# Windowed attention and feed-forward on one core: maxima from tiles of 32 queries of four heads, maxima and sums turned by VectorE, o stored by quadrant

## What is computed

```python
q = (x @ Wq.T).reshape(Bb, Tt, H, HD).transpose(0, 2, 1, 3)
k = (x @ Wk.T).reshape(Bb, Tt, H, HD).transpose(0, 2, 1, 3)
v = (x @ Wv.T).reshape(Bb, Tt, H, HD).transpose(0, 2, 1, 3)
attend = (|i - j| <= 128) | (i == 0) | (j == 0)
logits = where(attend, einsum('bhqd,bhkd->bhqk', q, k) / sqrt(HD), -inf)
out = einsum('bhqk,bhkd->bhqd', softmax(logits), v)
return out @ Wo.T
```

## Time and profile before

| | us |
|---|---|
| median of 3 runs | 1153.32 |
| lowest, highest | 1152.99, 1154.62 |
| span of the profiled execution | 1152.4 |
| attention, first shift row to last (L1347) | 193.0 to 759.1 |

### The profile page before, as it was taken

The page is one execution under the profiler, slowest core; times in us unless marked ns, Lnnn a source line. Parts: engine busy times, 40 slices in busy tenths (PEclk is TensorE's granted clock), DMA queues, the critical chain, the costliest instruction groups (busy, mean ns, idle before and its releaser), DMA issues.

```text
span 1152.4 us, 26576 instructions
## 1 busy us (share of the span) xinstructions
PE 1126.9 (98%) x9115; PEld 785.0 (68%) x9115; DVE 979.5 (85%) x3169; ACT 843.4 (73%) x1513; POOL 706.8 (61%) x935
## 2 busy tenths in 40 slices
PE   9999997999999999999999999999999999999998
PEld 8888884455555555555555455558888988898887
DVE  7889857899889998899889999867888888888885
ACT  7989983788888888888788888875465546554654
POOL 3665565677778777887778877773344334433443
PEclk9999998999999999999999999999999999999999
DMA  6999897555555555545565554240232113211201
GB/s 199 295 296 281 257 266 168 114 131 118 137 133 122 132 125 136 132 115 137 126 138 130 114 138 108 68 139 29 74 102 64 56 55 102 64 55 56 74 20 37
DMA packets 158166, 145.24 MB, mean 126 GB/s; under 512 B 21564, under 2 KB 157776, under 8 KB 158032
## 3 DMA queue, kind: packets, MB, share of 16 engines
q1 hardware_dynamic: 158032, 143.54, 48.8%
HBM read 91.74 MB, written 50.95 MB: 124 GB/s over the span
## 4 chain that ended last, share of the span: by engine, by line
PE 73%; DVE 7%; issue 2%; ACT 1%; POOL 1%; DVEq 0%; POOLq 0%; ACTq 0%
PE e_psum L1549 15%; PE e_psum L1503 15%; PE e_psum L1527 14%; PE e_psum L1844 6%; PE e_psum L1846 5%; PE e_psum L1267 3%; PE e_psum L1825 3%; PE e_psum L1824 3%; DVE n_stats L142 2%; DVE f_x L1958 2%; PE e_psum L1829 1%; PE e_psum L255 1%; PE e_psum L254 1%; PE e_psum L253 1%; PE e_psum L1793 1%
## 5 line engine op out<-in xcount | busy, mean ns | idle before, releaser
L1665 DVE CUSTOM_DVE_ANT_0 a_masked<-e_psum,band 128x387 f32<-128x387 f32 (+1 forms) x1024 | 493.3, 534 | 58.8 <-PE e_psum L1503 55.8
L1622 ACT ACTIVATE a_weights<-e_psum 128x1024 f32<-128x1024 f32 (+1 forms) x512 | 398.0, 806 | 87.2 <-PE e_psum L1527 82.2
L1401 POOL TENSOR_SCALAR_AFFINE_SELECT a_weights<-a_weights 128x1024 f32<-128x1024 f32 x256 | 276.2, 1091 | 59.9 <-ACT a_weights L1622 58.7
L1503 PE MATMUL e_psum<-e_k,e_q 96*128 96x387 bf16 (+1 forms) x1024 | 281.4, 327 | 3.0 <-PEq L281 1.4
L1888 POOL TENSOR_TENSOR f_square<-f_relu 128x512 f32<-128x512 f32 x128 | 146.1, 1142 | 209.6 <-ACT f_relu L1877 198.6
L1527 PE MATMUL e_psum<-e_q,e_k 128*128 128x384 bf16 (+2 forms) x1408 | 255.6, 279 | 1.5 <-ACT a_weights L1622 1.1
L1549 PE MATMUL e_psum<-a_weights,a_v 128*17 128x384 f32 (+2 forms) x2816 | 195.8, 392 | 1.0 <-POOL a_weights L1401 1.0
L1527 PEld LDWEIGHTS e_psum<-e_q,e_k 128*128 128x128 bf16 x1408 | 129.0, 98 | 95.6 <-issue 39.5
L1503 PEld LDWEIGHTS e_psum<-e_k,e_q 96*128 96x128 bf16 x1024 | 100.4, 98 | 99.2 <-DVE a_max L1665 44.8
L1844 PE MATMUL e_psum<-w_w_t,f_square_hi 128*128 128x256 f32 x512 | 129.4, 287 | 5.6 <-DVE f_square_lo L1934 5.6
L1846 PE MATMUL e_psum<-w_w_t,f_square_lo 128*128 128x256 f32 x512 | 126.8, 282 | 0.0
(11 more groups left out here) (219 smaller groups left out, 2059.0 us busy)
## 6 DMA issues: line engine op xcount, KB each, us to landing
k_parts<-p_k_parts SPq DMA_DIRECT2D x48, 258.0 KB, 4.6
e_k<-k_parts SPq DMA_DIRECT2D x64, 193.5 KB, 3.6
e_k<-k_parts SPq DMA_DIRECT2D x192, 64.5 KB, 3.3
q_parts<-p_q_parts SPq DMA_DIRECT2D x48, 256.0 KB, 5.1
e_q<-q_parts SPq DMA_DIRECT2D x64, 192.0 KB, 3.7
e_q<-q_parts SPq DMA_DIRECT2D x192, 64.0 KB, 3.3
v_ones<-p_va SPq DMA_DIRECT2D x16, 544.0 KB, 5.9
p_x<-in_x SPq DMA_DIRECT2D x16, 512.0 KB, 6.3
```

Source lines behind the costliest of these rows:

```text
L1401: pool.affine_select(out=blocks, in_=blocks, compare_op=ALU.is_ge, fill=0.0, base=0, pattern=[[0, NQ // 2 * HEAD_COLS // P // CUT_STEP], [ ...
L1503: pe.matmul(sh.tile_bank(ux, j)[:, lo:hi], qw[ux.q][0:SLOT_ROWS, h, t * P:t * P + P], kt[ux.hq][0:SLOT_ROWS, h, start + lo:start + hi], st ...
L1622: act.activation(pe_w[:, us.upar, lo:hi], score[c % 2][:], ACT.Exp).then_inc(s_exp, 1)
L1665: dve.tensor_tensor_reduce(out=masked[:, ux.upar, h, t:t + hi - lo], in0=bank[:, lo:hi], in1=band[:, lo:hi], scale=1.0, scalar=NEG, op0=AL ...
```

## The change

Maxima are now found in tiles of 32 queries of all four heads. A tile is four matmuls of 32 queries each, to partitions 0, 32, 64 and 96 of one bank, and has 290 columns in place of 387, since 32 neighbouring queries see fewer keys than 128. There are still 16 tiles in a unit. The mask `band` has the new shape, and is put together by 12 small operations of POOL (3 before) before the stage begins.

Since a tile's column of `mx` now holds 32 queries of four heads, VectorE can turn the maxima in 32x32 blocks (`mt`), and the sums as well, straight from the bank of the sums (`dve_sums_turned`). TensorE's transposes of both and ScalarE's two copies go. The turned maxima lie on four groups of 16 partitions, one for each head, so that each of the three parts is written by four DMAs. The four heads of a unit are now heads hq, hq+4, hq+8 and hq+12; o is laid out by quadrant and stored in four DMAs (eight in a sequence's first group), and v of key 0 comes in four. Two score banks come ahead of the first tile in TensorE's order, and POOL takes the denominators, the sums and the part of key 0 before LOW.

```diff
-WINDOW = 3 * KPITCH
+SUB = 32
+SUBS = GT // SUB
+QUADS = P // SUB
+WINDOW = 2 * P + SUB + 2
+BAND_DONE = 1 + 1 + 2 * QUADS
...
-TILES = NQ * TB
-
...
-TURN_OF_TILE = tuple(j + (j >= TURN_OF_M) + (j >= TURN_OF_S - 1) for j in range(TILES))
-TILE_OF_TURN = {k: j for j, k in enumerate(TURN_OF_TILE)}
-TURNS = TILES + 2
...
+STORES = (3 * QUADS, 2 * QUADS)
+
+BEFORE_TILES = (("score", 0), ("score", 1))
 AFTER_TILE = (
-    (("M", 0), ("score", 0), ("score", 1)), (), (("S", 0),), (("score", 2),),
-    (("score", 3),), (("score", 4),), (), (("sum", 0), ("score", 5)),
-    (), (), (("score", 6), ("score", 7)), (("score", 8), ("sum", 1), ("sum", 2)),
-    (("score", 9),), (("score", 10), ("score", 11)), (), (("sum", 3), ("sum", 4), ("sum", 5)))
+    (), (("score", 2),), (), (), (("score", 3), ("score", 4), ("score", 5)),
+    (), (), (("sum", 0),), (("score", 6), ("score", 7), ("sum", 1)),
+    (), (("sum", 2),), (("score", 8), ("score", 9), ("score", 10)),
+    (), (), (("sum", 3), ("score", 11), ("sum", 4)), (("sum", 5),))
...
+    def dve_sums_turned(self, dve, u):
+
+        dve.wait_ge(self.s_sum, u.n + 1)
+        wait(dve, self.s_den, u.n - 1)
+        wait(dve, self.s_num, u.n - 1)
+        dve.transpose(self.turned[:, u.upar].rearrange("p b e -> p (b e)"), self.sum_bank).then_inc(self.s_turned, 1)
...
+        mx, mt = sb("max", [P, UPG, SUB]), sb("max_turned", [P, SUB])
         d0 = sb("d0", [P, 2, TILES])
-        rest = sb("neg_rest", [TILES, P])
-        shift = sb("shift", [TILES, 2, SHIFT_ROWS, P], BF16)
+        rest = sb("neg_rest", [P, SUB])
+        shift = sb("shift", [P, 2, SHIFT_ROWS, SUB], BF16)
         pe_w = sb("weights", [P, 2, NQ * HEAD_COLS])
         score, sum_bank = sh.score, sh.sum_bank
         weights.move(ident, sh.banks[0:3] + [sum_bank])
...
+        def keys_of(gi, j):
+
+            start = (gi * TB + j // QUADS - 1) * KPITCH + 1 + j % QUADS * SUB
             return start, max(0, -start), min(WINDOW, KROW - start)
+
+        def key0_scores(u):
+
+            return bass.AP(masked, KEY0 + u.upar * TB * KPITCH,
+                           [masked[:].ap[0], [KPITCH, TB], [MASKED - SUB, QUADS]])
+
+        def masked_place(u, j):
+
+            t, quad = divmod(j, QUADS)
+            return quad * MASKED + (u.upar * TB + t) * KPITCH
 
         def window(gi):
 
...
-                        sp.dma_start(row.rearrange("s h (t q) -> s (h t) q", q=P),
-                                     shift[:, u.upar, part, :]).then_inc(s_row[u.upar], DMA)
+                        for h in range(NQ):
+                            row = qw[u.q][SLOT_ROWS + part:SLOT_ROWS + part + 1, h, :]
+                            sp.dma_start(row.rearrange("s (b r) -> s b r", r=SUB),
+                                         shift[h * SUB:h * SUB + SUBS, u.upar, part, :]
+                                         ).then_inc(s_row[u.upar], DMA)
                 if (u := at(L_SHIFT)) and u.hq == 0:
 
...
-                                 ).then_inc(s_v0[u.hq], DMA)
+                    for j in range(QUADS):
+                        h = j * UPG + u.hq
+                        sp.dma_start(v0[j * SUB:(j + 1) * SUB, u.hq],
+                                     va_dram[bass.ds(u.batch * T, 1), h * VW:(h + 1) * VW].to_broadcast((SUB, VW))
+                                     ).then_inc(s_v0[u.hq], DMA)
 
                 if (u := at(0)) and u.n >= PRELOADED:
                     wait(sp, s_score, (u.n - Q_BUFS) * CHUNKS + CHUNKS)
...
-                    if u.gi == 0:
-                        sp.dma_start(dst[1:P, 0], ob[1:P, u.gpar, 0]).then_inc(s_out[u.gpar], DMA)
-                        sp.dma_start(dst[:, 1:TB], ob[:, u.gpar, 1:TB]).then_inc(s_out[u.gpar], DMA)
-                    else:
-                        sp.dma_start(dst, ob[:, u.gpar]).then_inc(s_out[u.gpar], DMA)
+                    for j in range(QUADS):
+                        dst, src = sh.rows_of(o_dram, u.g, j), ob[j * SUB:(j + 1) * SUB, u.gpar]
+                        if u.gi == 0:
+                            sp.dma_start(dst[1:SUB, 0], src[1:SUB, 0]).then_inc(s_out[u.gpar], DMA)
+                            dst, src = dst[:, 1:SUBS], src[:, 1:SUBS]
+                        sp.dma_start(dst, src).then_inc(s_out[u.gpar], DMA)
 
             march(body, L_OUT)
 
...
+                    pool.wait_ge(s_turned, uo.n + 1)
+                    pool.tensor_tensor(den[:, uo.upar], turned[:, uo.upar, :, HD], p0[:, uo.p0], ALU.add
+                                       ).then_inc(s_den, 1)
+                    pool.tensor_tensor(num[:, uo.upar], turned[:, uo.upar, :, 0:HD], t0[:, uo.n % 3], ALU.add
+                                       ).then_inc(s_num, 1)
+                if us:
+
+                    pool.wait_ge(s_p0, us.n + 1)
+                    if us.gi == 0:
+                        pool.tensor_tensor(p0[:, us.p0], p0[:, us.p0], gate0[:], ALU.mult).then_inc(s_gate, 1)
+                        pool.wait_ge(s_gate, us.batch * UPG + us.hq + 1)
+                        pool.wait_ge(s_v0[us.hq], (us.batch + 1) * QUADS * DMA)
+                    wait(pool, s_num, us.n - 2)
+                    pool.tensor_tensor(
+                        t0[:, us.n % 3], v0[:, us.hq, 0:HD].unsqueeze(1).broadcast_to([P, SUBS, HD]),
+                        p0[:, us.p0].unsqueeze(2).broadcast_to([P, SUBS, HD]), ALU.mult).then_inc(s_t0, 1)
                 if um:
                     pool.wait_ge(s_mid, um.n + 1)
                     pool.tensor_tensor(shift[:, um.upar, LOW, :], rest[:], shift[:, um.upar, MID, :], ALU.subtract
...
-                    t, h = divmod(j, NQ)
-                    start, lo, hi = keys_of(ux.gi, t)
-                    pe.matmul(sh.tile_bank(ux, j)[:, lo:hi],
-                              qw[ux.q][0:SLOT_ROWS, h, t * P:t * P + P],
-                              kt[ux.hq][0:SLOT_ROWS, h, start + lo:start + hi], start=True, stop=True
-                              ).then_inc(s_tile, 1)
+                    wait(pe, s_tile_read, ux.n * TILES + j + 1 - TURN_BANKS)
+                    start, lo, hi = keys_of(ux.gi, j)
+                    for h in range(NQ):
+                        ins = pe.matmul(sh.tile_bank(j)[h * SUB:(h + 1) * SUB, lo:hi],
+                                        qw[ux.q][0:SLOT_ROWS, h, j * SUB:(j + 1) * SUB],
+                                        kt[ux.hq][0:SLOT_ROWS, h, start + lo:start + hi], start=True, stop=True)
+                    ins.then_inc(s_tile, 1)
 
                 def score_bank(n):
 
...
                             pe.wait_ge(s_ones[us.hq], 1)
-                        pe.wait_ge(s_row[us.upar], (us.uhalf + 1) * DMA * SHIFT_ROWS)
+                        pe.wait_ge(s_row[us.upar], (us.uhalf + 1) * DMA * SHIFT_ROWS * NQ)
                     if third == 0:
...
                         act.wait_ge(s_d0, um.n + 1)
                         wait(act, s_den, um.n + 1 - P0_BUFS)
-                        act.activation(p0[:, um.p0].rearrange("p h t -> p (h t)"), d0[:, um.upar, :], ACT.Exp
-                                       ).then_inc(s_p0, 1)
+                        act.activation(p0[:, um.p0], d0[:, um.upar, :], ACT.Exp).then_inc(s_p0, 1)
                 if uo and uo.n == UNITS - 2:
                     feed.act_norm_high(act, Group(0))
                 if um and um.n == 0:
...
             def body(at):
                 ux, um, uo = at(L_MAX), at(L_SHIFT), at(L_OUT)
+                if um:
+                    dve.wait_ge(s_tile_read, um.n * TILES + TILES)
+                    wait(dve, s_rest, um.n)
+                    dve.transpose(mt[:], mx[:, um.hq, :]).then_inc(s_m, 1)
+                if uo and uo.n < UNITS - 2:
+                    sh.dve_sums_turned(dve, uo)
                 for j in range(TILES):
-                    if um and j == 1:
+                    if um and j == 4:
                         dve.wait_ge(s_high, um.n + 1)
                         wait(dve, s_low, um.n)
-                        dve.scalar_tensor_tensor(out=rest[:], in0=sh.maxima_bank(um)[0:TILES, 0:P], scalar=-1.0,
+                        dve.scalar_tensor_tensor(out=rest[:], in0=mt[:], scalar=-1.0,
                                                  in1=shift[:, um.upar, HIGH, :], op0=ALU.mult, op1=ALU.subtract
                                                  ).then_inc(s_rest, 1)
                     if ux:
-                        t, h = divmod(j, NQ)
-                        start, lo, hi = keys_of(ux.gi, t)
-                        bank, c = sh.tile_bank(ux, j), h * TB + t
+                        start, lo, hi = keys_of(ux.gi, j)
+                        bank, place = sh.tile_bank(j), masked_place(ux, j)
                         if j == 0:
                             wait(dve, s_d0, ux.n - 1)
+                        if j == TILES - QUADS:
+                            wait(dve, s_d0, ux.n)
                         dve.wait_ge(s_tile, ux.n * TILES + j + 1)
 
                         dve.tensor_tensor_reduce(
```

(41 more changed lines are left out.)

202 lines of the change are left out of this document (66 added, 136 removed).

## The result

The changed kernel takes 1483.58 us at the median of four runs (1480.34 to 1487.38) against 1153.97 us of four of the kernel before (1152.99 to 1154.8): ratio 1.2865, 95% interval 1.284 to 1.2889. The forecast was 1400 us with a range of 1305 to 1470. The sign and the mechanism were right, the size was 84 us short.

The account below looks back on a forecast made before the run. SP's DMA queue was to bound the attention, the stage taking 802 us in place of 566. 1152.4 profiled, + 236 stage, + 15 clock, - 4 behind the last row = 1399; with 0.9 for the median 1400 us, range 1305 to 1470.

Parts of the forecast that it names:

- The bound: In the attention, SP's DMA queue would never idle and would set the step at 12.7 us.
- I take 0.575, the price of their own row: On SP's queue, each of 768 shift rows would cost 0.575 us to issue with its gap, 442 us.
- from above: Upper price of a shift row on SP's queue, one that follows close on another: 0.63 us.
- The list's 404 us: SP's issue time over the stage of the kernel before, its DMAs counted at the forecast's prices: 404 us.
- the waits view: SP's working time in the kernel before's stage, from its waits between 300 and 760 us: 402 us, taken as confirming the prices.
- The other terms of the list: SP's issues besides shift rows: k and q loads 264 us, v 10, v of key 0 38, stores of o 38.
- The last steps' latency: In the last seven steps, with few or no loads, SP's waiting would show: 10 us more in all.
- The clock, +15: PE, idle in part of each step, would get a lower clock in the stage: 15 us more.
- What PE and DVE gain: In the attention, PE's step would fall from 8.99 to 8.2 us, DVE's from 8.1 to 7.4, spent waiting for rows.
- Rival 2: SP keeps up, with issues below 0.28 us, and the change is faster: 1103 us, down to 1053; chance 0.04.
- Rival 3: A tile's four matmuls run one after the other, 0.5 us a tile: 1470 to 1540 us; chance 0.07.
- the stretches outside the stage: Time outside the stage: two shorter steps behind the last shift row would save 4 us.

Follow-up runs that it names:

- e1: The kernel before, with each shift row written by four DMAs of 32 columns in place of one of 128: 1412.73 us, ratio 1.225.
- e3: The changed kernel with only the rows of the first two of four heads written, six DMAs in a unit: 1243.52 us, ratio 1.0783.
- e5: The changed kernel with v of key 0 loaded once in a sequence by four DMAs, 48 issues less: 1457.75 us, ratio 1.2649.
- e8: e6 with stores of o spread over four steps, rounding of the maxima behind the fourth tile and their turn behind the fifth: 1159.77 us, ratio 1.0063.
- e2: The changed kernel with HIGH's four row DMAs issued by ScalarE, the other eight by SP: 1454.86 us, ratio 1.2616.
- e6: The changed kernel with e5's loads and maxima rounded to bf16, so one shift row replaces three, four row DMAs a unit: 1160.48 us, ratio 1.0078.
- e12: e8 with the rows of heads 2 and 3 issued by ScalarE behind its third exponential: 1165.27 us, ratio 1.0099.
- e4: The changed kernel with only the first head's rows written, three DMAs in a unit: 1157.95 us, ratio 1.0045.

## Why the prediction missed

- **The bound: right.** SP's queue never idle, waits for HIGH and MID gone from it, PE held at the start of each step by a shift row, DVE and ACT below 70%, the clock below 1.00, the stages around it within 4 us: all are in the profile after, and e1, e3 and e5 move the time by about the price of the issues that they add or leave out. The step is 14.1 us, not the 12 to 13 that were to show it.
- **The step that failed: "I take 0.575, the price of their own row".** A shift row cost 0.676 us with its gap (768 took 518.8), and 768 x 0.10 = 77 of the 84 us are there. There were two errors in it. First, 0.532 is what a row costs behind a wait or behind another kind of DMA. Right behind another row it costs 0.59, the new median, as e8's chain shows: 0.53 for the first, which stands behind a store without a wait, and 0.59 for the next. The trace of before had both: of its 192 rows 62 stood right behind another and took 0.590, the median of the rest was 0.53. This is 0.057 us, 44 us for 768 rows. The prediction named this value, 0.63 with the gap, and used it only as the upper end. Second, a median leaves out the long issues. In the change 49 of the 768 rows took over 0.8 us, and they lift the mean to 0.633, which is another 33 us, and that with its gap to 0.676, above the end called "from above".
- **The check that seemed to cover it was chance.** The list's 404 us met 402 from the waits view, "stragglers of over 1 us included". Issue by issue, SP was busy for 428.7 us of the 566 and idle 137.4: the waits view, scaled to the stage, had put its idle time at 164, which is 27 too much, and the list was 25 short. The rows' own 192 took 118.7 us, not the 110 of the list. Long issues, over 0.8 us, are no fixed share: 35 of 719 before, 70 of 1400 after, but 69 of 837 in e8.
- **The other terms of the list: near.** Loads 276.7 us for 264, v 10.0 for 10, v of key 0 31.9 for 38, stores 43.1 for 38; together 361.7 for 350. The last steps' latency was put at 10 us; SP idled 9.4 in the stage, of which some 6 in the last steps.
- **The clock, +15: nothing.** It fell as far as feared, to 0.83, and cost nothing: PE's 10.0 us of work at that clock still fit into 14.1. (In e2, where PE is the bound, it does cost.) The term had been added to a sum whose bound was another engine. Without it the miss is 15 us larger, so the row's price does not explain it alone: from 1399, the sum for the span, -15 for the clock, +77 for the rows, +12 for the other terms, and +9 for the stretches outside the stage (put at -4, measured +5.4) make 1482.
- **What PE and DVE gain: right in size.** DVE was put at 7.4 us a step and works 7.6; the turned sums were taken at 0.69. The tile fell by 95 ns where 99 was the estimate.
```profile
L1642 DVE CUSTOM_DVE_ANT_0 a_masked<-e_psum,band 128x290 f32<-128x290 f32 x896 | 374.5, 456 | 320.9 <-PE e_psum L1481 312.7
...
L1276 DVE STREAM_TRANSPOSE e_turned<-e_psum 128x512 f32<-128x512 f32 x64 | 44.2, 691 | 4.6 <-PE e_psum L1527 4.6
```
- PE was put at 8.2 and needs 8.3 to 8.4 when nothing holds it (e6, e8).
- **Rival 2's arithmetic was too kind.** It had 1103 us if SP kept up. With four rows a unit SP does keep up, and seven versions (e6 to e12) gave 1159 to 1189. A step in which PE works 8.3 us and DVE 7.8 leaves each little slack to wait for the other, for the row's 3.3 us, or for POOL; this is argued from the waits, of which no run takes away all. Its condition, an issue below 0.28 us, did not hold in any run: the shortest row took 0.502. The Trainium skill, "DMA: Bandwidth & Descriptors", section Anatomy of one DMA, has about 50 ns for the dispatch of a transfer issued by GpSimd; nothing SP issued here came near it.
- **Rival 3** (tile matmuls one after the other, 1470 to 1540) had the right time by the wrong mechanism: a tile takes 0.127 us.

Still open: why one issue in 12 to 20 takes 0.8 to 2 us, and whether an order exists that brings the shorter step of e8 into the time of the whole kernel; twelve runs did not find one.

## What to carry to other kernels

Count the DMAs that a queue issues in a step as you count matmuls, and price them by the mean of issues that follow on one another, gaps and long ones included: a median of issues that mostly had waited, or stood behind another kind, is too low. A change of layout that splits one transfer into four, because the partitions no longer line up, can cost more than all the compute that it saves. Where the bound is a queue, add nothing for engines that stay below it; and where two engines fill 88% and 94% of a step, a saving on both has to get past every hand-over between them before it shows. Look at the length of a regular step beside the time of the whole: a gain there can be lost in the first and last steps.

## What the runs showed of the hardware

- A row of 1 KB costs SP what one of 4 KB does (the median is 532 ns in e4 and in the kernel before), and 0.59 us when it stands right behind another row, with 0.04 between issues. The number counts, not the size.
- Four 32-row matmuls into the four quadrants of a bank pass in 0.127 us for 290 columns; a change from such a tile to scores, which fill all 128 partitions of a bank at once, costs 0.11, one from a tile to sums nothing that these rows show.
- The same VectorE operation of 128x16, the rounding, took 0.71 us in the mean in e6, where it stands right behind the tile that wrote its input's last column, and 0.40 in e8, where it stands four tiles later. Its place is not the whole cause: single ones took from 0.17 to 1.12 us in e8. What lengthens them is open.
- A landing of a row took 1.7 us at the median in the change and 3.27 in the step of e8 above, right behind eight loads and a store of 64 KB to 194 KB each.
